# One matmul per key block for the exponents of two heads: mask, key part and running maximum in one operand, split on ScalarE and GpSimd and laid out through DRAM, with new orders on the engines

## The chip, the cores and the metric

The kernel runs on one core of one Trainium2 chip. The metric is the device time of one execution in microseconds. The kernel before takes 1728.18 us, the median of 3 runs (1726.94 to 1734.21).

## What is computed

Input x is (128, 256, 512) and a context of the same shape: 128 batches of 256 positions and 512 features, 8 heads of 64. A layer norm of x gives the queries; keys and values are the context itself. The first layer is a gated linear attention:

```python
ig, fg = gi @ igate_w.T + igate_b, gi @ fgate_w.T + fgate_b   # gi = [q, k, v]
cs = cumsum(log_sigmoid(fg))
log_D = where(tril, cs[:, None] - cs[None, :], -inf) + ig[None, :]
D = exp(log_D - max(log_D, -1))
C = (q @ k.T / 8) * D
h = (C / (max(|sum C|, exp(-max)) + 1e-6)) @ v
x = x + layernorm_per_head(h) * out_w
x = x + fp8_gemm(layernorm(x)) + bias
```

With a = ig - cs per key and a running maximum mx of a per query, the exponent of D for a key and a later query is a(key) - mx(query), and it is masked where the key comes after the query. These exponents, for each head, are what the change makes in another way.

## The kernel before, in words

The batches go through a software pipeline. Every engine has a function slot(m), called for m from FIRST to B + LAST, which issues one piece of each stage for batches m - 4 to m + 10; the engines don't share a clock, they are tied by semaphores only, and each works its slot's list in the order in which it is written. One period is the time in which every engine does the work of one batch.

What one batch needs, with the lines of the profile:

- SP issues all DMAs (the context c_sb and its halves c_first, the keys kT, x twice: for the norm, x_sb, and for the residual, into o_sb; store writes o_sb out, L336). load_own (L304) loads x into the buffer that the output leaves from, so it waits until the store of two batches earlier has landed, and all of SP's queue behind it waits with it.
- ScalarE normalises x; TensorE turns it (turn, L391), ScalarE keeps it as qT; gates (L402) gives the gate sums.
- Once per group of four batches the scans run, on 32 rows (4 batches x 8 heads) of 256 columns: scan_rows on TensorE (L416), abs, exp, log, relu on ScalarE, three scans and a few sums on VectorE. am holds a in columns 0 to 255 and mx in 256 to 511. scan_rest (L1048, VectorE, twice per group) takes from am its upper 16 bits and then again, so that rows 0 to 31, 32 to 63 and 64 to 95 hold three pieces of which each fits in bf16: a sum of three bf16 operands gives the fp32 value.
- arg(b, q), on TensorE, four times per batch, makes the exponents of two heads in one PSUM bank: 14 bf16 matmuls (L445 to L457) in three kinds. am is the stationary operand and the head's selector hsel the moving one for a; hsel_neg is stationary and am moving for -mx; ident_bf and the table later add -1e30 where the key comes after the query. Operands of 64 columns come in pairs (low and high half of the output partitions) that run side by side.
- ScalarE takes the exponential (decay, L613), VectorE multiplies it with the scores (matrix, L909, from scores, L476), TensorE multiplies that with the values (within, L508), adds what comes across the two halves (across, L520; states, L488), VectorE adds and normalises per head (L916 to L955), GpSimd scales and adds the residual (head_norm L1143, scale_heads L1156, residual L1161; weigh_keys L1134 weights the keys for states).
- The second norm (L963 to L980), its bf16 turn (L531), the quantisation to fp8 on ScalarE (quantise, L746, once per batch), the feed-forward product in the one PSUM bank y (ffn, L545 and L547, twice per batch) and finish (L1003, VectorE, after each of the two).

At the start SP loads the first four batches and the weights; VectorE then rounds the feed-forward weights (L847 to L867) between its first slots and waits for w_out before it.

The few lines that carry the stages:

```python
mm(low[:, :, 0:2, :], tops[:, 0:Q], two, start=True, stop=False)            # arg, L445, a of the lower keys
mm(low[:, h, 0:2, :], neg, tops[:, S:S + 2 * Q], start=False, stop=False)   # L451, -mx
mm(low[:, :, 0::2, :], ident_bf[:, 0:Q], later..., start=False, stop=True)  # L455, the mask
tt(am[(n + 1) * R:(n + 2) * R, g, :], rows, top, ALU.subtract)              # scan_rest, L1048
```

## Time and profile before

| | |
|---|---|
| median of 3 runs | 1728.18 us (1726.94 to 1734.21) |
| the profiled execution | 1743.25 us |
| its span | 1741.5 us |
| TensorE busy | 1598.6 us, 92% |
| VectorE busy | 1548.9 us, 89% |
| ScalarE busy | 1282.7 us, 74% |
| GpSimd busy | 1104.4 us, 63% |
| moved by DMA | 377.66 MB, mean 217 GB/s |

The span is the time from the first to the last instruction of one execution; the profiled execution's own time is 1.75 us more. Busy counts a moment once, also when two instructions of an engine overlap in it. Shares are over the whole span, fill and drain included, so that windows of the steady middle tell more. A row of the trace gives the start and the duration of an instruction; TensorE's matmuls are pipelined, and the distance from start to start is what one costs. PE is TensorE, PEld its weight load, DVE VectorE, ACT ScalarE, POOL GpSimd, SPq SP's queue of DMA issues.

### The profile page before, as it was taken

Reading aid. Unit: us, or ns where it says so; the run is one execution under the profiler, and the core shown is the slowest. Engines: PE = TensorE matmul, PEld = TensorE weight load, DVE = VectorE, ACT = ScalarE, POOL = GpSimd, SP = SyncE. Lnnn points to the kernel's source line nnn. Section 1 sums busy time; section 2 is a strip of 40 time slices with the busy share of each in tenths; the row PEclk is TensorE's granted clock in tenths of the full one; section 3 lists DMA queues with packets and bytes.
Section 4 is the critical chain, followed back from the end, with each engine's and each line's share of the span. In section 5 each row is a group of like instructions: output and inputs, shape, how many; then the busy total and the mean of one; then the engine's idle time right before and its main releaser. Section 6 shows DMA issues by size and latency. Waiting matters only on the chain.

```text
span 1741.5 us, 88634 instructions
## 1 busy us (share of the span) xinstructions
PE 1598.6 (92%) x36224; PEld 1191.2 (68%) x36224; DVE 1548.9 (89%) x4157; ACT 1282.7 (74%) x3137; POOL 1104.4 (63%) x1036
## 2 busy tenths in 40 slices
PE   2779999999999999999999999999999999999985
PEld 1567777776777776777776767777777777777662
DVE  6679999999998999999999999999999899998884
ACT  3667877777787777777877778777777787777652
POOL 0056766666666666666666667766666666666774
PEclk9899999999999999999999999999999999999996
DMA  5557778777777677677776777778778777776542
GB/s 164 198 168 220 249 222 237 222 230 231 224 237 233 218 234 226 214 240 221 238 235 216 227 233 227 244 217 246 218 225 240 216 223 241 230 232 195 179 130 73
DMA packets 164022, 377.66 MB, mean 217 GB/s; under 512 B 15008, under 2 KB 16032, under 8 KB 163616
## 3 DMA queue, kind: packets, MB, share of 16 engines
q1 hardware_dynamic: 163616, 371.96, 69.2%
q8 instruction: 290, 4.75, 1.1%
q14 instruction: 116, 0.95, 0.2%
HBM read 304.79 MB, written 67.11 MB: 214 GB/s over the span
## 4 chain that ended last, share of the span: by engine, by line
PE 58%; DVE 21%; issue 9%; DMA 9%; ACT 2%; POOL 1%; DVEq 0%; SPq 0%; POOLq 0%; ACTq 0%
PE work L508 9%; PE y L547 9%; PE qk L476 8%; PE turn L391 6%; PE turn L402 5%; DMA o_sb<-in_x 5%; DVE dec L909 4%; DMA out<-o_sb 3%; DVE bn L963 3%; DVE o_sb L1003 3%; PE arg L445 3%; PE work L488 3%; PE y L531 2%; PE y L545 2%; DVE am L1048 2%
## 5 line engine op out<-in xcount | busy, mean ns | idle before, releaser
L1143 POOL TENSOR_TENSOR x<-x,h_r 128x512 f32<-128x512 f32 x256 | 269.3, 1052 | 261.4 <-DVE x L955 146.0
L1156 POOL TENSOR_TENSOR x<-x,w_out 128x512 f32<-128x512 f32 x256 | 360.2, 1407 | 20.1
L1161 POOL TENSOR_TENSOR x<-x,o_sb 128x512 f32<-128x512 f32 x256 | 321.2, 1276 | 38.5 <-DMA o_sb<-in_x 38.2
L508 PEld LDWEIGHTS work<-c_first,dec 128*64 128x64 f32 x4096 | 264.7, 138 | 69.2 <-issue 69.0
L508 PE MATMUL work<-c_first,dec 128*64 128x65 f32 x4096 | 290.9, 224 | 12.2 <-issue 4.8
L508 PE MATMUL work<-c_sb,dec 128*64 128x65 f32 x4096 | 292.3, 224 | 2.4 <-issue 2.3
L508 PEld LDWEIGHTS work<-c_sb,dec 128*64 128x64 f32 x4096 | 264.7, 138 | 5.3 <-issue 5.3
L476 PE MATMUL qk<-qT,kT 64*64 64x128 f32 (+1 forms) x8192 | 236.0, 250 | 34.6 <-DVE dec L909 28.6
L547 PE MATMUL y<-w_ffn,zq 128*128 128x512 bf16 x1024 | 267.2, 384 | 0.0
L1003 DVE SCALAR_TENSOR_TENSOR o_sb<-y,s_out,x 128x512 f32<-128x512 f32 x256 | 190.4, 744 | 78.1 <-PE y L547 77.2
L613 ACT ACTIVATE dec<-arg 128x384 f32<-128x384 f32 x512 | 243.2, 475 | 19.4 <-PE arg L457 18.7
L909 DVE TENSOR_TENSOR dec<-qk,dec 128x768 f32<-128x768 f32 x256 | 242.8, 948 | 8.0 <-PE qk L476 8.0
L476 PEld LDWEIGHTS qk<-qT,kT 64*64 64x64 f32 x8192 | 198.9, 133 | 69.0 <-issue 41.3
L946 DVE BATCH_NORM_STATS2 bn_h<-g_sb 128x6 f32<-128x128 f32 x1024 | 224.0, 280 | 0.0
L649 ACT ACTIVATE q_nat<-x_sb,nb,r 128x512 f32<-128x512 f32 x256 | 205.5, 806 | 0.0
L738 ACT ACTIVATE z_bf<-x,nb,r 128x512 bf16<-128x512 f32 x256 | 194.5, 807 | 14.2 <-DVE nb L980 11.3
L391 PE MATMUL turn<-ident,q_nat 128*128 128x128 f32 x1024 | 173.5, 293 | 28.9 <-ACT q_nat L649 19.3
L963 DVE BATCH_NORM_STATS2 bn<-x 128x6 f32<-128x512 f32 x256 | 174.5, 681 | 18.4 <-POOL x L1161 18.0
L746 ACT ACTIVATE zq<-y,s_inv 128x1024 fp8e4<-128x1024 bf16 x128 | 142.5, 1113 | 59.9 <-PE y L531 59.9
L885 DVE BATCH_NORM_STATS2 bn<-x_sb 128x6 f32<-128x512 f32 x256 | 174.6, 683 | 13.5 <-DMA x_sb<-in_x 6.7
L955 DVE TENSOR_TENSOR x<-g_sb,bn_h 128x512 f32<-128x512 f32 x256 | 183.1, 715 | 1.0
L601 ACT ACTIVATE qT<-turn 128x512 f32<-128x512 f32 x256 | 151.5, 592 | 36.9 <-PE turn L391 31.7
(120 smaller groups left out, 4547.8 us busy)
## 6 DMA issues: line engine op xcount, KB each, us to landing
c_sb<-in_ctx SPq DMA_DIRECT2D x128, 520.0 KB, 6.2
x_sb<-in_x SPq DMA_DIRECT2D x128, 512.0 KB, 5.1
kT<-in_keys SPq DMA_DIRECT2D x128, 512.0 KB, 6.6
o_sb<-in_x SPq DMA_DIRECT2D x128, 512.0 KB, 4.6
out<-o_sb SPq DMA_DIRECT2D x128, 512.0 KB, 3.1
c_first<-in_ctx SPq DMA_DIRECT2D x256, 130.0 KB, 5.3
w_ffn<-in_L_ffn_kernel SPq DMA_DIRECT2D x1, 512.0 KB, 10.1
w_out<-in_L_xattn_out_w SPq DMA_DIRECT2D x1, 256.0 KB, 11.7
```

What stands on the lines that cost most here:

```text
L391: last = turn(turn_ps[:, (T * c + t) * P:(T * c + t + 1) * P], q_nat[:, t, chunk * P:(chunk + 1) * P], ident[:, :])
L476: last = mm(out[0:Q, u, to, :] if lower else out[Q:P, u, to, :], kT[half, r, c, key * Q:(key + 1) * Q], qT[half, r, c, query * Q:(query + ...
L508: last = mm(work_ps[rows, u, c * W:(c + 1) * W], heads_dec[:, slot * Q:(slot + 1) * Q], src, start=True, stop=True)
L547: last = mm(y_ps, (zq_wide if wide_z else zq)[:, c, t * P:(t + 1) * P], w_ffn[:, c, :], start=False, stop=c == C - 1)
L613: af(dec[:, b.k % 2, q, :], arg_ps[:, 0:U * HEAD], ACT.Exp).then_inc(decays[q].sem, 1)
L909: tt(mine, qk_ps[:, :, 0:U * HEAD], mine, ALU.mult).then_inc(weighted[p].sem, 1)
L946: done = ve.bn_stats(bn_h[:, first:first + U, :].rearrange("p u k -> p (u k)"), g_sb[:, b.k % 2, t, c, 1:1 + U * DH].rearrange("p (u d) -> ...
L963: done = ve.bn_stats(bn2[:, t, :], x1[:, b.k % 2, t, :])
L1003: stt(o_sb[:, b.k % 2, t, :], y_ps, s_out[:, :], x1[:, b.k % 2, t, :], ALU.mult, ALU.add).then_inc(out_set[t].sem, 1)
L1143: pl.tensor_tensor(h, h, h_r[:, t * NH:(t + 1) * NH].unsqueeze(2).broadcast_to([P, NH, DH]), ALU.mult).then_inc(h_normed[t].sem, 1)
L1156: pl.tensor_tensor(h, h, w_out[:, :], ALU.mult).then_inc(h_scaled[t].sem, 1)
L1161: pl.tensor_tensor(x1[:, b.k % 2, t, :], x1[:, b.k % 2, t, :], o_sb[:, b.k % 2, t, :], ALU.add).then_inc(x1_set[t].sem, 1)
```

## The change

1. Three pieces of a and mx are now made once per group by ScalarE and GpSimd: parts_high (ScalarE copies am to bf16), scan_rest (GpSimd subtracts), parts_middle (ScalarE copies), parts_low (GpSimd subtracts). VectorE's scan_rest is gone, am has 32 rows.
2. SP stores the pieces to DRAM, once per group with four DMAs (store_parts): the keys' as they are, the queries' into an image in which a head's piece stands only in its own columns, and other heads' columns stay zero. Per batch it loads both back (load_parts): 24 rows of 256 (arg_keys) and 24 rows of 3072 (arg_queries), two buffers of each.
3. The operands for arg have 112 rows: 64 with the identity against the mask, 24 with a's pieces against ones in the head's own columns, 24 with -1 against mx's pieces. One matmul of a key block does what three kinds did, so arg is 4 matmuls instead of 14.
4. At the start SP loads the constant rows of both buffers, and the images in DRAM are filled from the same table; SP waits for these six DMAs before it issues the feed-forward weights.
5. The orders of all five slots are new, and FIRST and LAST are one further out on either side.

```diff
-FIRST, LAST = -10, 4
+FIRST, LAST = -11, 5
...
-        am = sb("am", [P, 2, 2 * S])
+        am = sb("am", [R, 2, 2 * S])
+        rest = sb("rest", [R, 2 * S])
+        parts = sb("parts", [R, 3, 2 * S], bf16)
+        arg_keys = sb("arg_keys", [ROWS, PART_RING, S], bf16)
+        arg_queries = sb("arg_queries", [ROWS, PART_RING, NH, SPAN], bf16)
+        key_parts = nc.dram_tensor("key_parts", (2, GROUP, NH, 3, S), bf16).ap()
+        query_parts = nc.dram_tensor("query_parts", (2, GROUP, IMAGE), bf16).ap()
...
+            def store_parts(b):
+                g = b.k // GROUP % 2
+                sp.wait_ge(*parts_set.of(b))
+                if b.follows(2 * GROUP):
+                    for last in range(1, PART_RING + 1):
+                        before = b - (GROUP + last)
+                        sp.wait_ge(parts_in[before.k % PART_RING], before.count(32, 32, PART_RING))
+                sp.dma_start(key_parts[g, :, :, :, :].rearrange("j h n s -> (j h) n s"), parts[:, :, 0:S]).then_inc(parts_stored, 16)
+                for to, at, n in ((0, 0, S), (S, Q, Q), (S + Q, 3 * Q, Q)):
+                    sp.dma_start(own_columns(g, to, n), parts[:, :, S + at:S + at + n]).then_inc(parts_stored, 16)
+
+            def load_parts(b):
+                r, g, j = b.k % PART_RING, b.k // GROUP % 2, b.k % GROUP
+                sp.wait_ge(parts_stored, b.count(N_PARTS, N_PARTS, GROUP))
+                if b.follows(PART_RING):
+                    sp.wait_ge(*args[3].of(b - PART_RING))
+                sp.dma_start(arg_keys[KEY_ROWS, r, :], key_parts[g, j, :, :, :].rearrange("h n s -> (h n) s")).then_inc(parts_in[r], 16)
+                sp.dma_start(arg_queries[QUERY_ROWS, r, :, :].rearrange("p h s -> p (h s)"),
+                             image(g, j)).then_inc(parts_in[r], 16)
 
...
+            for r in range(PART_RING):
+                sp.dma_start(arg_keys[:, r, :], c_keys).then_inc(blank_in, 16)
+                sp.dma_start(arg_queries[:, r, :, :].rearrange("p h s -> p (h s)"), c_queries).then_inc(blank_in, 16)
+            for g in range(2):
+                sp.dma_start(query_parts[g, :, 0:PARTS * NH * SPAN],
+                             c_queries[QUERY_ROWS, :].rearrange("p n -> (p n)").unsqueeze(0).broadcast_to([GROUP, PARTS * NH * SPAN])).then_inc(blank_in, 16)
+            sp.wait_ge(blank_in, N_BLANK)
...
             def slot(m):
+                if live(m - 5):
+                    store(m - 5)
+                if live(m + 6):
+                    load_keys(m + 6)
+                if scans(m):
+                    store_parts(m)
+                if live(m - 1):
+                    load_first(m - 1)
+                if live(m - 3):
+                    load_own(m - 3)
+                if live(m):
+                    load_parts(m)
+                if live(m + 2):
+                    load_c(m + 2)
                 if live(m + 10):
                     load_x(m + 10)
-                if live(m - 2):
-                    load_own(m - 2)
-                if live(m + 7):
-                    load_keys(m + 7)
-                if live(m + 1):
-                    load_first(m + 1)
-                if live(m + 3):
-                    load_c(m + 3)
-                if live(m - 3):
-                    store(m - 3)
 
...
             def arg(b, q):
-
-                j, g = b.k % GROUP, b.k // GROUP % 2
-                row = j * NH + 2 * U * (q // U) + q % U
-                tops = am[:, g, :].bitcast(bf16).rearrange("p (s two) -> p s two", two=2)[:, :, 1]
-                mine = hsel[:, row:row + U + 1:U]
+                r = b.k % PART_RING
+                first = 2 * U * (q // U) + q % U
+                mine = slice(first, first + U + 1, U)
                 out = arg_ps[:, 0:U * HEAD].rearrange("p (h s n) -> p h s n", h=2, s=3)
                 low, high = out[0:Q], out[Q:P]
                 if q == 0:
-                    pe.wait_ge(*rest_set[1].of(b))
-                    if not b.follows(1):
-                        pe.wait_ge(dve_set, N_SCAN_SET)
+                    pe.wait_ge(parts_in[r], b.count(32, 32, PART_RING))
                     if b.follows(1):
                         pe.wait_ge(*decays[3].of(b - 1))
                 else:
                     pe.wait_ge(*decays[q - 1].of(b))
-                two = mine.unsqueeze(2).unsqueeze(3).broadcast_to([P, 2, 2, Q])
-                one = mine.unsqueeze(2).broadcast_to([P, 2, Q])
-                mm(low[:, :, 0:2, :], tops[:, 0:Q], two, start=True, stop=False)
-                mm(high[:, :, 0::2, :], tops[:, 2 * Q:3 * Q], two, start=True, stop=False)
-                mm(low[:, :, 2, :], tops[:, 3 * Q:4 * Q], one, start=False, stop=False)
-                mm(high[:, :, 1, :], tops[:, Q:2 * Q], one, start=False, stop=False)
-                for h in range(2):
-                    neg = hsel_neg[:, row + U * h:row + U * h + 1].broadcast_to([P, Q])
-                    mm(low[:, h, 0:2, :], neg, tops[:, S:S + 2 * Q], start=False, stop=False)
-                    mm(high[:, h, 0::2, :], neg, tops[:, S + 2 * Q:S + 4 * Q], start=False, stop=False)
-                    mm(low[:, h, 2, :], neg, tops[:, S + 3 * Q:S + 4 * Q], start=False, stop=False)
-                    mm(high[:, h, 1, :], neg, tops[:, S + Q:S + 2 * Q], start=False, stop=False)
-                mm(low[:, :, 0::2, :], ident_bf[:, 0:Q], later[:, 0:Q].unsqueeze(1).unsqueeze(2).broadcast_to([P, 2, 2, Q]),
-                   start=False, stop=True)
-                mm(high[:, :, 0:2, :], ident_bf[:, Q:P], later[:, Q:P].unsqueeze(1).unsqueeze(2).broadcast_to([P, 2, 2, Q]),
-                   start=False, stop=True).then_inc(args[q].sem, 1)
+                tops = arg_queries[:, r, mine, :].rearrange("p h (s n) -> p h s n", n=Q)
+                mm(low[:, :, 0:2, :], arg_keys[:, r, 0:Q], tops[:, :, 0:2, :], start=True, stop=True)
+                mm(high[:, :, 0::2, :], arg_keys[:, r, 2 * Q:3 * Q], tops[:, :, 2:4, :], start=True, stop=True)
+                mm(low[:, :, 2, :], arg_keys[:, r, 3 * Q:4 * Q], tops[:, :, 5, :], start=True, stop=True)
+                mm(high[:, :, 1, :], arg_keys[:, r, Q:2 * Q], tops[:, :, 4, :], start=True, stop=True).then_inc(args[q].sem, 1)
 
...
             def slot(m, wide_z):
+                if live(m + 2):
+                    arg(m + 2, 3)
+                if live(m - 1):
+                    ffn(m - 1, 0, wide_z)
+                if live(m + 9):
+                    turn_round(m + 9, 0)
+                if live(m + 2):
+                    states(m + 2)
+                if live(m - 1):
+                    ffn(m - 1, 1, wide_z)
+                if live(m + 9):
+                    turn_round(m + 9, 1)
                 if live(m + 3):
                     arg(m + 3, 0)
-                if scans(m + 3):
-                    scan_turn(m + 3)
-                if live(m + 9):
-                    turn_round(m + 9, 1)
-                if live(m - 1):
-                    ffn(m - 1, 1, wide_z)
                 if live(m + 2):
...
+            def parts_high(b):
+                act.wait_ge(*max_set.of(b))
+                if b.follows(GROUP):
+                    act.wait_ge(parts_stored, b.count(N_PARTS, 0, GROUP))
+                af(parts[:, 0, :], am[:, b.k // GROUP % 2, :], ACT.Copy).then_inc(high_set.sem, 1)
+
+            def parts_middle(b):
+                act.wait_ge(*rest_set.of(b))
+                af(parts[:, 1, :], rest[:, :], ACT.Copy).then_inc(middle_set.sem, 1)
...
-            def scan_rest(b, n):
-
-                g = b.k // GROUP % 2
-                dve.wait_ge(*(rest_set[0] if n else max_set).of(b))
-                if b.follows(2 * GROUP):
-                    dve.wait_ge(*args[3].of(b - (GROUP + 1)))
-                rows = am[n * R:(n + 1) * R, g, :]
-                top = rows.bitcast(bf16).rearrange("p (s two) -> p s two", two=2)[:, :, 1]
-                tt(am[(n + 1) * R:(n + 2) * R, g, :], rows, top, ALU.subtract).then_inc(rest_set[n].sem, 1)
...
+            def scan_rest(b):
+                pool.wait_ge(*high_set.of(b))
+                if b.follows(GROUP):
+                    pool.wait_ge(*parts_set.of(b - GROUP))
+                pl.tensor_tensor(rest[:, :], am[:, b.k // GROUP % 2, :], parts[:, 0, :], ALU.subtract).then_inc(rest_set.sem, 1)
+
+            def parts_low(b):
+                pool.wait_ge(*middle_set.of(b))
+                pl.tensor_tensor(parts[:, 2, :], rest[:, :], parts[:, 1, :], ALU.subtract).then_inc(parts_set.sem, 1)
...
             def slot(m):
                 if live(m + 7):
+                    scale_heads(m + 7, 0)
+                    scale_heads(m + 7, 1)
+                if scans(m + 11):
+                    scan_rest(m + 11)
+                if live(m + 8):
+                    head_var(m + 8)
+                if live(m + 7):
+                    residual(m + 7, 0)
                     residual(m + 7, 1)
+                if scans(m + 11):
+                    parts_low(m + 11)
                 if live(m + 10):
                     weigh_keys(m + 10)
                 if live(m + 8):
                     head_norm(m + 8, 0)
-                    scale_heads(m + 8, 0)
                     head_norm(m + 8, 1)
-                    scale_heads(m + 8, 1)
-                if live(m + 9):
-                    head_var(m + 9)
-                if live(m + 8):
-                    residual(m + 8, 0)
 
...
+    block, parts = P // 2, 3 * n_heads
+    own = np.repeat(np.eye(n_heads, dtype=np.float32), 3, axis=0)
+    earlier = np.where(np.arange(block)[:, None] > np.arange(block)[None, :], np.float32(-1e30), np.float32(0))
+    keys = np.zeros((block + 2 * parts, 4, block), np.float32)
+    keys[:block] = np.eye(block, dtype=np.float32)[:, None, :]
+    keys[block + parts:] = -1
+    queries = np.zeros((block + 2 * parts, n_heads, 6, block), np.float32)
+    for masked in (0, 2, 4, 5):
+        queries[:block, :, masked, :] = earlier[:, None, :]
+    queries[block:block + parts] = own[:, :, None, None]
```

TensorE, in the steady run, from the second transpose of a batch over the first feed-forward half to arg. Before (the names: turn is the transposes' and gates' bank, y the feed-forward's, work the states'):

```order
L391 MATMUL turn<-ident,q_nat 128x128 x4
L545 MATMUL y<-b_parts,b_rows 128x512
L547 MATMUL y<-w_ffn,zq 128x512 x4
L488 MATMUL work<-c_sb,k_w 64x65 x8
L445 MATMUL arg<-hsel,am 64x2x128
L446 MATMUL arg<-hsel,am 64x2x2x64
L447 MATMUL arg<-hsel,am 64x2x64
L448 MATMUL arg<-hsel,am 64x2x64
L451 MATMUL arg<-am,hsel_neg 64x128
L452 MATMUL arg<-am,hsel_neg 64x2x64
L453 MATMUL arg<-am,hsel_neg 64x64
L454 MATMUL arg<-am,hsel_neg 64x64
```

Six more rows of arg follow there. Now:

```order
L581 MATMUL y<-b_parts,b_rows 128x512
L583 MATMUL y<-w_ffn,zq 128x512 x4
L442 MATMUL turn<-ident,q_nat 128x128 x4
L524 MATMUL work<-c_sb,k_w 64x65 x8
L581 MATMUL y<-b_parts,b_rows 128x512
L583 MATMUL y<-w_ffn,zq 128x512 x4
L442 MATMUL turn<-ident,q_nat 128x128 x4
L491 MATMUL arg<-arg_queries,arg_keys 64x2x128
L492 MATMUL arg<-arg_queries,arg_keys 64x2x2x64
L493 MATMUL arg<-arg_queries,arg_keys 64x2x64
L494 MATMUL arg<-arg_queries,arg_keys 64x2x64
```

arg is whole in these four rows. The first call of a batch now comes after both feed-forward halves, and between the two halves stand a transpose and the states.

SP, the slot in which a group's pieces are stored. Before, a slot was:

```order
L336 DMA out_0<-o_sb 128x2x512
L295 DMA x_sb<-in_x 128x2x512
L304 DMA o_sb<-in_x 128x2x512
L320 DMA kT<-in_keys 128x1024
L332 DMA c_first<-in_ctx 64x520 x2
L314 DMA c_sb<-in_ctx 128x1040
```

Now, once per group (in the other three slots L362 and L364 are missing):

```order
L377 DMA out_0<-o_sb 128x2x512
L341 DMA kT<-in_keys 128x1024
L362 DMA key_parts<-parts 96x1x256
L364 DMA query_parts<-parts 32x3x256
L364 DMA query_parts<-parts 32x3x64 x2
L353 DMA c_first<-in_ctx 64x520 x2
L325 DMA o_sb<-in_x 128x2x512
L371 DMA arg_keys<-key_parts 24x256
L372 DMA arg_queries<-query_parts 24x3072
L335 DMA c_sb<-in_ctx 128x1040
L316 DMA x_sb<-in_x 128x2x512
```

The loads of the pieces come behind the residual's load, and so behind the landing of the store at the top.

GpSimd, the same group's slot, now (h_r, w_out and o_sb name head_norm, scale_heads and residual):

```order
L1197 TENSOR_TENSOR x1<-x1,w_out 128x512 x2
L1174 TENSOR_TENSOR rest<-am,parts 32x512
L1192 TENSOR_TENSOR h_v<-h_n2,bn_h 128x16
L1202 TENSOR_TENSOR x1<-x1,o_sb 128x512 x2
L1178 TENSOR_TENSOR parts<-rest,parts 32x512
L1165 TENSOR_TENSOR k_w<-c_sb,facs 128x512
```

The two subtractions (L1174, L1178) stand ahead of the keys' weighting and around the residual; the rest of the slot is as long as it was.

## Rows read from the trace of the kernel before

**Rows 1.** Page: the span; busy us of each engine (share of the span) xinstructions.

```profile
span 1741.5 us, 88634 instructions
...
PE 1598.6 (92%) x36224; PEld 1191.2 (68%) x36224; DVE 1548.9 (89%) x4157; ACT 1282.7 (74%) x3137; POOL 1104.4 (63%) x1036
```

**Rows 2.** Windows, 400 to 1472 us: busy us per engine, granted clock, DMA share.

```profile
core 0: us, PE busy (x) PEld busy (x) DVE busy (x) ACT busy (x) POOL busy (x), PEclk, DMA share, GB/s
400.00:1472.00 1072.00, 1023.57 (x23634) 769.62 (x23629) 991.29 (x2672) 831.75 (x2043) 717.03 (x668) 1.00 0.75 229
```

**Rows 3.** Line L746 between 600 and 1100 us: count, duration, first and last start.

```profile
L746 ACT ACTIVATE zq<-y,s_inv x39: 1113/1113/1115, 599.5 to 1088.4; 128x1024 fp8e4<-128x1024 bf16 x39
```

**Rows 4.** Waits, 400 to 1472 us: us in total, times, longest.

```profile
PE qk L476 <- DVE dec L909: 18.9, 18, 1.1
...
DVE o_sb L1003 <- PE y L547: 39.4, 46, 2.2
```

**Rows 5.** Timeline of TensorE: start us, duration us, what; one call of arg.

```profile
814.35 0.27 PE L445 MATMUL arg<-hsel,am 128*64 128x256 bf16 x1
...
814.46 0.22 PE L447 MATMUL arg<-hsel,am 128*64 128x128 bf16 x1
...
814.52 0.22 PE L451 MATMUL arg<-am,hsel_neg 128*64 128x128 bf16 x1
...
814.70 0.27 PE L455 MATMUL arg<-later,ident_bf 128*64 128x256 bf16 x1
...
814.90 0.90 PE L476 MATMUL qk<-qT,kT 64*64 64x128 f32 x32
```

**Rows 6.** VectorE's subtractions: group (busy, mean ns), then least, median, greatest ns.

```profile
L1048 DVE TENSOR_TENSOR am<-am 32x512 f32<-32x512 f32 x64 | 75.2, 1175 | 2.0
...
L1048 DVE TENSOR_TENSOR am<-am x64: 680/702/1799, 60.5 to 1652.2; 32x512 f32<-32x512 f32 x64
```

**Rows 7.** Timelines of VectorE and of GpSimd at 829 us.

```profile
829.52 1.79 DVE L1048 TENSOR_TENSOR am<-am 32x512 f32<-32x512 f32 x1
...
829.49 1.28 POOL L1156 TENSOR_TENSOR x<-x,w_out 128x512 f32<-128x512 f32 x1
```

**Rows 8.** Groups: finish on VectorE, and those nearest to the added operations; busy, mean ns.

```profile
L1003 DVE SCALAR_TENSOR_TENSOR o_sb<-y,s_out,x 128x512 f32<-128x512 f32 x256 | 190.4, 744 | 78.1 <-PE y L547 77.2
...
L601 ACT ACTIVATE qT<-turn 128x512 f32<-128x512 f32 x256 | 151.5, 592 | 36.9 <-PE turn L391 31.7
...
L1134 POOL TENSOR_TENSOR k_w<-c_sb,facs 128x512 f32<-128x512 f32 x128 | 133.7, 1044 | 70.3 <-ACT facs L697 62.4 <-PE work L488 7.9
...
L1161 POOL TENSOR_TENSOR x<-x,o_sb 128x512 f32<-128x512 f32 x256 | 321.2, 1276 | 38.5 <-DMA o_sb<-in_x 38.2
```

**Rows 9.** Timeline of SP's queue: start us, time to issue, what.

```profile
814.26 0.40 SPq L336 DMA_DIRECT2D out<-o_sb  x1
...
817.30 0.37 SPq L304 DMA_DIRECT2D o_sb<-in_x  x1
```

**Rows 10.** Waits of SP, 400 to 1472 us.

```profile
SPq L304 <- DMA out<-o_sb: 203.1, 84, 4.5
```

**Rows 11.** Page, DMA issues: KB each, median us from issue to landing.

```profile
kT<-in_keys SPq DMA_DIRECT2D x128, 512.0 KB, 6.6
...
out<-o_sb SPq DMA_DIRECT2D x128, 512.0 KB, 3.1
c_first<-in_ctx SPq DMA_DIRECT2D x256, 130.0 KB, 5.3
```

**Rows 12.** The fill: a window, VectorE's wait and first maximum, ScalarE's first exponential.

```profile
12.00:22.00 10.00, 2.05 (x8) 1.43 (x8) 6.50 (x22) 3.30 (x8) 0.00 (x0) 1.00 0.90 320
...
21.59 0.41 DVE L847 MEMSET b_rows<- 1x128 bf16 x2 [1.23 <-DMA w_out<-in_L_xattn_out_w]
...
59.16 0.66 DVE L1028 TENSOR_TENSOR_SCAN am<-am 32x256 f32<-32x256 f32 x1
...
66.36 0.49 ACT L613 ACTIVATE dec<-arg 128x384 f32<-128x384 f32 x1 [0.22 <-PE arg L457]
```

174 lines of the change are left out of this document (86 added, 88 removed).

## The prediction, before the change was run

> **What bounds the kernel now.** I read the page first: on the whole span TensorE is busy 92% and VectorE 89% [rows 1]. An average over fill, steady run and drain does not say which of the two sets the pace, so the next view was a window over the steady middle: 1072 us in which TensorE ran at its full granted clock (1.00 of 2.4 GHz) and the DMA engines were busy 0.75 of the time [rows 2]. One ScalarE operation happens once per batch (the quantisation); 39 of them start between 599.5 and 1088.4 us, so a batch takes 488.9 / 38 = 12.87 us [rows 3] and the window holds 1072 / 12.87 = 83.3 batches. Per batch the engines are then busy: TensorE 1023.57 / 83.3 = 12.29 us, VectorE 991.29 / 83.3 = 11.90, ScalarE 9.98, GpSimd 8.61 [rows 2]. So TensorE is the limit with 0.58 us of idle time a batch, and VectorE stands only 0.39 us behind it. The waits agree: VectorE's largest wait in that window is for TensorE's feed-forward product, 39.4 us or 0.47 a batch, while TensorE's largest, for VectorE, is 18.9 us [rows 4]. 128 batches at 12.87 are 1647 us; the other 94 us of the span are fill and drain.
>
> **TensorE: the exponents.** Today each of the four calls of arg per batch is 14 matmuls. In the timeline the call starts at 814.35, its third matmul (after the first pair of 256 columns) at 814.46, the last pair at 814.70, and the next operation starts at 814.90: 0.55 us [rows 5]. The change keeps the first pair (0.11 us) and one pair of 128 columns, after which the scores follow. That last pair costs at least the 0.06 us of a pair of 128 columns between its neighbours, and at most the 0.20 us that the last pair of 256 now takes before the scores; I take 0.14. The call then takes 0.25, and saves 0.30 us; four of them save **1.2 us a batch**, bounds 0.24 x 4 = 0.96 and 0.38 x 4 = 1.5. TensorE's need falls from 12.29 to about 11.1 us. It is no longer the limit, so this is not the gain.
>
> **VectorE: the splits go away.** scan_rest was two subtractions per group of four batches, 64 in all, 75.2 us, mean 1175 ns [rows 6]. Over 128 batches that is **0.59 us a batch**. VectorE's need falls from 11.90 to 11.3 us, and it becomes the limit. Nothing else on it is removed; the other moves only reorder. That the mean is 1175 and the shortest 680 ns [rows 6] is worth a look: one of 1.79 us started 0.03 us after a GpSimd multiplication that ran 1.28 us [rows 7]. The subtraction sat waiting for GpSimd. The Trainium skill (SBUF — State Buffer, Who interferes with whom) says that VectorE's second port pair is shared with GpSimd as an exclusive lock, taken for a whole instruction, also against VectorE operations with two SBUF inputs. The trace agrees.
>
> **ScalarE and GpSimd take the splits over.** Two copies of 32x512 per group on ScalarE: a Copy of 128x512 takes 592 ns, so 2 x 0.6 / 4 = 0.3 us a batch, to 10.3. Two subtractions on GpSimd, between the 1044 and the 1276 ns of its 512-element operations [rows 8]: 0.52 to 0.64, taken as 0.58, to 9.2 us. Both stay more than 1 us below VectorE, and I cost them at nothing; if they hit VectorE through the port of rows 7, that is a rival below.
>
> **DMA and SP's queue.** Each batch adds loads of 24x512 bytes and 24x6144 bytes, 160 KB, and each group four stores, about 123 KB: 0.19 MB on top of 2.9 MB. DMA busy time of 0.75 x 12.87 = 9.6 us [rows 2, 3] becomes about 10.2; at a 12 us batch that is 0.85 of the time. No limit, but the landings will hardly be shorter, and the piece of 147 KB sits on 24 partitions only, with its share of the engines unknown: evenly spread it adds 0.34 us to each, if a third of the engines carry it 1 us to those. The serial path counts more. On SP, the part loads of batch b stand behind: the store of b-5 (0.40 us), the residual load, which waits until that store has landed (3.1), its issue (0.37), and two issues of their own (0.4 each) [rows 9, 11]. SP already waits so: 203.1 us in the window for the store's landing [rows 10]. With VectorE's 0.74 us to finish b-5 [rows 8], and a landing L of the parts, arg(b, 0), about one period later on TensorE, asks for a period of at least 0.74 + 0.40 + 3.1 + 0.37 + 0.8 + L = 5.4 + L. The nearest row for L is the load of c_first, 130 KB, 5.3 us [rows 11]: 10.7 us, hidden. For the first batch of a group four stores (1.6 us to issue) and the wait for their landing come in between: 12.3 us, just late, and more if GpSimd's last piece comes late itself. For this and for landings above 5.3 us I charge **0.2 us a batch**, between 0 (all hidden) and what rival D gives.
>
> **The period.** No engine runs without waits here: today the limiting one idles 0.58 us per batch. I give VectorE the same: 11.3 + 0.58 + 0.2 = **12.1 us**. From below 11.3 bounds it; from above nothing here does, and the rivals say what would push it up. 128 x (12.87 - 12.1) = **-99 us**.
>
> **The fill gets longer.** SP now issues six loads of constants, the masked blanks, and waits for all of them before the feed-forward weights. They are 2 x (57 + 688) KB into SBUF and 2 x 590 KB within DRAM, 2.7 MB; the DMA engines moved 320 GB/s at 12 to 22 us, at 0.90 busy [rows 12]. So 8.4 us, plus a landing and the weights' own way after it, about 3: **+11 us**. Today VectorE's next step in the fill waits for w_out until 21.59 us [rows 12], so the delay counts in full. Less than 5 is excluded by the bytes; if the copies within DRAM go at half that rate, it is 15. The first group's splits then go ScalarE, GpSimd, ScalarE, GpSimd (0.6 + 1.05 + 0.6 + 1.05), DRAM stores (1.6 to issue, 3.1 to land) and loads (0.8 + 3 to 5): 12 to 14 us after the first running maximum at 59.16 + 0.66, so about 73 us. The first exponential starts now at 66.36 [rows 12]: **+7 us**. Together +18, bounds +8 and +30.
>
> **Sum**: -99 + 18 = -81 us. Against the profiled execution, 1743.25 us (span 1741.5 and 1.75 around it), that is 1662; the profiled run stands 15 us above the median of 1728.18, so for the median **1647 us**.
>
> **Rivals.**
> (A) VectorE hardly waits: TensorE, with 1.8 us more than it needs, always has its product ready. For it: 0.47 of today's 0.97 us of VectorE idle is waiting for that product [rows 4]. Against it: y is one bank, so finish and product still alternate. Period 11.5, fill +12: 1728 - 175 + 12 = 1565 us.
> (B) GpSimd gives it back. Its 0.58 us a batch of new subtractions each hold up a VectorE operation as in rows 7; at worst in full. Period 11.3 + 0.58 + 0.58 = 12.5: 1728 - 47 + 18 = 1699 us. For it: rows 7. Against it: the old subtraction, which suffered from the same, is gone. The rule of the Trainium skill named above asks for this case if its lock meets two-input operations each time.
> (C) The gain is swallowed whole: the once-a-group work of TensorE, ScalarE and VectorE now lies in different slots, and if each of them waits for the other's, their times add rather than overlap. 11.3 with 1.45 us of idle is 12.75: 1728 - 15 + 18 = 1731 us. Nothing in today's trace shows so much idle time.
> (D) **Slower**: the parts come late for every batch. This is SP's path with L as the one unknown: it decides against today's kernel from L = 12.87 - 5.4 = 7.5 us on. For it: the keys' load, 512 KB, has a median of 6.6 us [rows 11], the DMA engines become busier, and only 24 partitions hold the whole piece. At L = 8.3 the period is 13.7: 1728 + 106 + 18 = 1852 us. Against it: 130 KB took 5.3, and what stands in the queue ahead has mostly landed during SP's wait. The Trainium skill (SBUF — State Buffer, Door 1: the DMA port swizzle) states a rule that speaks for D: a transfer reaches only the ports that its partitions belong to, and by its table partitions 88 to 111 are six of sixteen. An estimate by that page: 147 KB / 6 = 24.6 KB for each of six engines, on top of some 180, so these would be busy 11 us or more of each batch, and the queues in front of them long. No run here shows the spread yet; the one load of 64 partitions, c_first, takes 5.3 us for a quarter of the bytes that the keys' takes 6.6 for.
>
> **Chances.** The forecast (1605 to 1690) 0.50; A 0.10; B 0.22; C 0.06; D 0.12. A measurement of this kernel tells about 0.5%, 8.6 us, from no change. Faster by more: 0.82; within it: C, 0.06; slower: D, 0.12. The range leaves out D and the lower half of A (periods under 11.6): 1575 to 1732 us.
>
> **What would show it.** Right: quantisations 12.1 us apart in the steady middle (11.8 to 12.4); arg at about 0.25 us from its start to the next operation; TensorE busy near 11.1 and VectorE near 11.3 us a batch, VectorE now the busier one; landing of the query parts under 6 us, and nearly no TensorE wait for them but one in four; VectorE's wait in the fill until about 33 us. Wrong: TensorE waits with the DMA of the parts as the releaser in every batch (D); GpSimd's or VectorE's two-input operations with means well above today's (B); VectorE idle above 1 us a batch with waits spread over slots (C); a period still near 12.9 with TensorE busy 12.3, which would mean that the small matmuls were not what took the time.

## The result, and the profile after

The changed kernel takes 1738.84 us (median of 20 runs), the kernel before 1733.32 in the same session: ratio **1.0037, 95% interval 1.0020 to 1.0055**. By the ratio that is 6.4 us slower (5.5 by the medians), less than the 0.5% that was called no change. The prediction was 1647 us and faster. All comparisons below are ratios to the kernel before on the same chip, since its median moved between 1727 and 1738 us from chip to chip; differences in us are differences of these ratios, and 1% is 17.3 us. Between runs on different chips the plain medians can give another size; where that matters, both are given.

The profiled execution took 1734.2 us (span 1732.4), 5 us under its own median, while the profiled one of before stood above its median; so this pair of profiles shows 9 us of gain where the medians show a loss of 6. Against [rows 1], the page:

```profile
span 1732.4 us, 79000 instructions
...
PE 1491.7 (86%) x31104; PEld 1073.4 (62%) x31104; DVE 1509.6 (87%) x4091; ACT 1311.8 (76%) x3201; POOL 1139.2 (66%) x1097
```

The window over the steady middle, against [rows 2], and the quantisations, against [rows 3]:

```profile
400.00:1472.00 1072.00, 973.61 (x20684) 707.64 (x20683) 980.23 (x2678) 867.81 (x2129) 754.84 (x723) 1.00 0.81 248
```

```profile
L793 ACT ACTIVATE zq<-y,s_inv x40: 1114/1115/1116, 607.1 to 1096.3; 128x1024 fp8e4<-128x1024 bf16 x40
```

In this stretch a batch takes 489.2 / 39 = 12.54 us. The 85 quantisations of the whole window (406.3 to 1465.8 us) are 12.61 us apart, so the window holds 85.0 batches: TensorE 11.46 us, VectorE 11.53, ScalarE 10.21, GpSimd 8.88. TensorE's busy time fell by 0.8 us (12.29 before; 1.2 forecast), VectorE's by 0.4 (11.90 before; 0.6 forecast), and VectorE now idles 1.08 us a batch.

A window is not the run, though. Over all 128 quantisations (groups of the two lines; before, then now) the distance is 12.73 us before and 12.51 now, 0.22 less, where the stretches of [rows 3] gave 0.33: 127 times 0.22 is 27 us, and the fill takes 18 of them back, which is the 9 us of this pair.

```profile
L746 ACT ACTIVATE zq<-y,s_inv x128: 1113/1113/1115, 114.7 to 1730.9; 128x1024 fp8e4<-128x1024 bf16 x128
```

```profile
L793 ACT ACTIVATE zq<-y,s_inv x128: 1114/1115/1117, 133.0 to 1721.8; 128x1024 fp8e4<-128x1024 bf16 x128
```

The call of arg shrank as forecast. What a call costs depends on what follows it. Where the scores follow, as in [rows 5], 0.55 us became 0.29 (825.39 to 825.68). Where the product with the values follows, it is now 0.19 us (824.26 to 824.45); before, such calls took 0.48:

```profile
824.26 0.30 PE L491 MATMUL arg<-arg_queries,arg_keys 112*64 112x256 bf16 x1
...
824.39 0.22 PE L494 MATMUL arg<-arg_queries,arg_keys 112*64 112x128 bf16 x1
824.45 0.22 PE L544 MATMUL work<-c_first,dec 128*64 128x65 f32 x1
...
825.39 0.30 PE L491 MATMUL arg<-arg_queries,arg_keys 112*64 112x256 bf16 x1
...
825.68 0.90 PE L512 MATMUL qk<-qT,kT 64*64 64x128 f32 x32
```

Three things in the trace stand out against the kernel before; what each is worth, the experiments have to say. First, VectorE's subtraction for the exponentials of the scans, 403 ns in the kernel before, now runs beside GpSimd's (timelines of VectorE and of GpSimd; group of the line: busy, mean ns):

```profile
825.47 1.49 DVE L1087 TENSOR_TENSOR ex<-ncs,am 32x256 f32<-32x256 f32 x1
```

```profile
825.53 1.15 POOL L1178 TENSOR_TENSOR parts<-rest,parts 32x512 bf16<-32x512 f32 x1
```

```profile
L1087 DVE TENSOR_TENSOR ex<-ncs,am 32x256 f32<-32x256 f32 x32 | 46.7, 1460 | 0.0
```

Second, DMAs land late. Of the waits in the window, these name a load (us in total, times, longest):

```profile
POOL x L1202 <- DMA o_sb<-in_x: 31.6, 31, 2.9
...
PEld arg L491 <- DMA arg_queries<-query_parts: 10.5, 14, 2.3
...
PE arg L491 <- DMA arg_queries<-query_parts: 7.4, 8, 2.0
```

The last two rows are the same moments twice, once for the weight load and once for the matmul behind it: 14 of the window's 85 first calls waited for the query parts, 10.5 us in all. The residual's x was waited for before too (22.1 us, 21 times).

Third, the fill. VectorE's wait for w_out, which ended at 21.59 us before [rows 12], ends at 41.75, behind the blanks (timeline of VectorE, and the chain that ended last):

```profile
41.75 0.66 DVE L895 MEMSET b_rows<- 1x128 bf16 x3 [21.71 <-DMA w_out<-in_L_xattn_out_w]
```

```profile
10.88 24.72 DMA query_parts<-in_c_queries
36.61 5.07 DMA w_out<-in_L_xattn_out_w
```

The first of the 128 quantisations starts at 132.99 us, 18.3 later than before (114.69). From the last one to the end it is 10.6 us in both.

### The profile page after: what moved, and what is told of

Same layout as the page of the kernel before. It is cut to its first block, busy times and chain, and to the rows that moved or that the text cites. A ratio compares the mean times of both kernels' runs of the same rounds, so it can differ in the third digit from the quotient of the medians.

```text
span 1732.4 us, 79000 instructions
## 1 busy us (share of the span) xinstructions
PE 1491.7 (86%) x31104; PEld 1073.4 (62%) x31104; DVE 1509.6 (87%) x4091; ACT 1311.8 (76%) x3201; POOL 1139.2 (66%) x1097
## 4 chain that ended last, share of the span: by engine, by line
PE 36%; DVE 24%; issue 15%; DMA 10%; ACT 8%; POOL 3%; SPq 3%; DVEq 0%; ACTq 0%; POOLq 0%
PE y L583 7%; PE work L544 6%; DMA o_sb<-in_x 4%; DVE dec L957 4%; DVE bn L1011 3%; PE qk L512 3%; PE turn L453 3%; PE y L567 3%; ACT zq L793 3%; PE y L581 3%; DVE o_sb L1051 3%; PE turn L442 2%; DVE bn_h L994 2%; DMA arg_queries<-query_parts 2%; POOL x L1202 2%
## 5 line engine op out<-in xcount | busy, mean ns | idle before, releaser
L544 PE MATMUL work<-c_first,dec 128*64 128x65 f32 x4096 | 286.4, 223 | 44.0 <-DVE carry L964 40.2
L1197 POOL TENSOR_TENSOR x<-x,w_out 128x512 f32<-128x512 f32 x256 | 321.3, 1277 | 0.0
L544 PEld LDWEIGHTS work<-c_first,dec 128*64 128x64 f32 x4096 | 260.5, 138 | 64.2 <-issue 62.5
L650 ACT ACTIVATE dec<-arg 128x384 f32<-128x384 f32 x512 | 247.4, 483 | 23.6 <-PE arg L494 22.8
L544 PEld LDWEIGHTS work<-c_sb,dec 128*64 128x64 f32 x4096 | 260.6, 138 | 1.2 <-issue 1.1
L512 PE MATMUL qk<-qT,kT 64*64 64x64 f32 (+1 forms) x8192 | 239.9, 251 | 17.6 <-issue 16.7
L638 ACT ACTIVATE qT<-turn 128x512 f32<-128x512 f32 x256 | 152.0, 594 | 124.5 <-PE turn L442 123.4
L442 PE MATMUL turn<-ident,q_nat 128*128 128x128 f32 x1024 | 162.5, 283 | 59.6 <-ACT q_nat L686 53.5
L442 PEld LDWEIGHTS turn<-ident,q_nat 128*128 128x128 f32 x1024 | 131.9, 146 | 113.2 <-ACT q_nat L686 57.2
L1011 DVE BATCH_NORM_STATS2 bn<-x 128x6 f32<-128x512 f32 x256 | 169.8, 682 | 23.9 <-POOL x L1202 23.5
L1003 DVE TENSOR_TENSOR x<-g_sb,bn_h 128x512 f32<-128x512 f32 x256 | 182.1, 711 | 0.5 <-issue 0.5
```

What stands on the lines that cost most here:

```text
L442: last = turn(turn_ps[:, (T * c + t) * P:(T * c + t + 1) * P], q_nat[:, t, chunk * P:(chunk + 1) * P], ident[:, :])
L512: last = mm(out[0:Q, u, to, :] if lower else out[Q:P, u, to, :], kT[half, r, c, key * Q:(key + 1) * Q], qT[half, r, c, query * Q:(query + ...
L544: last = mm(work_ps[rows, u, c * W:(c + 1) * W], heads_dec[:, slot * Q:(slot + 1) * Q], src, start=True, stop=True)
L650: af(dec[:, b.k % 2, q, :], arg_ps[:, 0:U * HEAD], ACT.Exp).then_inc(decays[q].sem, 1)
L1011: done = ve.bn_stats(bn2[:, t, :], x1[:, b.k % 2, t, :])
L1197: pl.tensor_tensor(h, h, w_out[:, :], ALU.mult).then_inc(h_scaled[t].sem, 1)
```

## The experiments

**What is the removed work worth?** Three versions of the kernel before.

b_four, the calls of arg:
```diff
-                mm(low[:, :, 0:2, :], tops[:, 0:Q], two, start=True, stop=False)
...
+                mm(low[:, :, 0:2, :], ident_bf[:, 0:Q], two, start=True, stop=True)
+                mm(high[:, :, 0::2, :], ident_bf[:, Q:P], two, start=True, stop=True)
+                mm(low[:, :, 2, :], ident_bf[:, 0:Q], one, start=True, stop=True)
+                mm(high[:, :, 1, :], ident_bf[:, Q:P], one, start=True, stop=True).then_inc(args[q].sem, 1)
```


> The kernel before with TensorE's relief alone: each exponent call issues four matmuls with the changed kernel's column counts (the identity as weights, so that the running maximum and the mask are left out of the exponents) in place of fourteen; VectorE, GpSimd, the DMAs and all orders stay. Theory TensorE (the matmuls' length sets the period together with VectorE, as the prediction's sum has it): 1.2 us a batch less on TensorE, but VectorE's 11.90 stays, so the period goes from 12.87 to some 12.5 and the run falls by about 50 us (40 to 60). Theory VectorE (TensorE had slack, its waits only move): less than 20 us.

b_norest, VectorE's slots (and arg waits for max_set):
```diff
-                if scans(m + 1):
-                    scan_rest(m + 1, 0)
...
-                    scan_rest(m + 1, 1)
```


> The kernel before with VectorE's relief alone: the two subtractions scan_rest of each group are left out (the exponents lack their middle and low pieces), nothing replaces them. Theory TensorE: TensorE's 12.29 stays, so the run falls by at most 20 us. Theory VectorE: 0.59 us a batch of VectorE's path goes, 128 times: the run falls by 40 to 75 us.

b_both, both edits:

> Both reliefs in the kernel before, with no GpSimd work, no DMA and no new order beside them (exponents without pieces, running maximum and mask). It is what the change removes, without what it adds. The prediction's steady term (12.87 to 12.1) says about 100 us less. If the removed work was worth less than that, the prediction's sum failed in what it took away; if it is 100 us or more, it failed in what the change adds.

Measured: b_four 1705.27 us, ratio 0.9805 (0.9776 to 0.9835), -34 us; b_norest 1712.52, 0.9842 (0.9813 to 0.9871), -27 us; b_both 1643.92, **0.9456 (0.9424 to 0.9487), -94 us**. The two together are worth 33 us more than their sum: with one engine relieved the other holds the period. Each alone is below what the theory of its own engine gave it (40 to 60, 40 to 75), and above the other theory. The window of b_both, and its wait for the residual's x:

```profile
400.00:1472.00 1072.00, 1007.07 (x21320) 716.30 (x21316) 981.66 (x2761) 871.74 (x2148) 763.43 (x702) 0.99 0.77 240
```

```profile
POOL x L1147 <- DMA o_sb<-in_x: 51.2, 34, 3.3
```

Its 88 quantisations in the window (399.6 to 1463.9 us) are 12.23 us apart, which gives VectorE 11.20 us a batch and 1.03 idle. The chain that ended last points to where much of that idle time comes from: in this window 14.8% of it is the load of the residual's x and 8.4% the store that this load waits for, against 3.2% and nothing listed in the kernel before; VectorE's own wait for the residual rose from 7.7 to 31.6 us. Of the 94 us about 7 are fill (first quantisation 108.0 against 114.7). So the change removes nearly what the prediction's steady term needed, and **all of it is given back by what the change adds and moves: 101 us** from b_both (0.9456) to the changed kernel (1.0037).

**Is TensorE's saving still used?** a_thrice issues the four matmuls three times:

> The changed kernel with each exponent call's four matmuls issued three times over into the same place (same result): TensorE gets back 0.5 us a call, 2 us a batch, 256 us in all. If TensorE is still what the batches wait for, the run grows by more than 150 us; if VectorE sets the period now and TensorE has its 1.15 us a batch of slack, by the 0.85 us a batch that goes beyond the slack, some 110 us or less. This tells how much of TensorE's saving the changed kernel still uses.

Measured: 1781.05, ratio 1.0237 (1.0209 to 1.0266), 35 us above the changed kernel. The expectation took 0.5 us more a call; the trace has 0.33 (a call before the product with the values takes 0.52 us in place of 0.19), so some 170 us of matmuls came in, and TensorE's busy time rose from 11.46 to 12.42 us a batch. Only 35 us show, 9 of them in the fill (first quantisation 142.2). So TensorE's matmuls do not set the period of the changed kernel. What is left is the busiest engine, VectorE, with its waits; a_exp and a_expool below take work from it.

**What does the change give back?** First the fill, a_wfirst:
```diff
+            sp.dma_start(w_ffn[:, :, :], ffn_w.rearrange("(c p) f -> p c f", p=P)).then_inc(weights_in, 16)
...
             for r in range(PART_RING):
                 sp.dma_start(arg_keys[:, r, :], c_keys).then_inc(blank_in, 16)
...
-            sp.wait_ge(blank_in, N_BLANK)
-            sp.dma_start(w_ffn[:, :, :], ffn_w.rearrange("(c p) f -> p c f", p=P)).then_inc(weights_in, 16)
```
SP waits for the blanks only ahead of the first store of parts.

> The changed kernel with the feed-forward weights, their bias and the output weights issued ahead of the DRAM images' blanks; SP waits for the blanks only ahead of the first store of parts. Theory fill (VectorE's 21.7 us wait for w_out until 41.75 is the fill's limit): w_out lands as before, near 30 us, and the run falls by 11 to 18 us. Rival (the first group's round trip through DRAM, arg at 94.0, sets the start whatever lands earlier): under 5 us.

Then the loads of the parts, a_noparts:
```diff
-                sp.wait_ge(parts_stored, b.count(N_PARTS, N_PARTS, GROUP))
                 if b.follows(PART_RING):
-                    sp.wait_ge(*args[3].of(b - PART_RING))
+                    return
+                sp.wait_ge(parts_stored, b.count(N_PARTS, N_PARTS, GROUP))
```
store_parts no longer waits for earlier loads, and arg waits only for the first two.

> The changed kernel without the loads of the key and query parts after the first two batches (all exponents are then made of the parts of those two): 252 of its DMAs gone, the stores into the DRAM image stay. Theory DMA (the parts' traffic and their lateness, with the residual's load that comes late by them, give back the gain): the waits for own_in and for the parts go, and the run falls by 40 to 80 us. Rival (the two-input clash of GpSimd and VectorE and the once-a-group work do it): under 15 us.

a_exp, VectorE's slots:
```diff
-                if scans(m + 1):
-                    scan_exponents(m + 1)
...
                 if scans(m + 2):
                     scan_max(m + 2)
+                    scan_exponents(m + 2)
```


> The changed kernel with VectorE's scan_exponents right behind scan_max, one batch earlier, where GpSimd makes no subtraction. If the clash of the two engines is what stretches its subtraction from 403 to 1460 ns, the mean of the line returns to about 400 to 600 ns, worth 1.0 us a group and up to 32 us in all if VectorE sets the period; by the theory that DMAs set it, under 8 us.

a_nosplit, GpSimd's slots:
```diff
-                if scans(m + 11):
-                    scan_rest(m + 11)
...
-                    parts_low(m + 11)
```
ScalarE's parts_middle copies am in place of rest.


> The changed kernel without GpSimd's two subtractions a group (the middle piece is a copy of the high one and the low one stays zero); ScalarE's copies, the stores, the loads and the orders stay. Theory port (GpSimd's 74 us of subtractions hold up VectorE's two-input operations and GpSimd's own chain to the residual): the run falls by 25 to 60 us. Theory DMA: under 15 us.

Measured: a_wfirst 0.9998 (0.9975 to 1.0021), 7 us under the changed kernel, with intervals that just touch, so between the two theories; in the trace the fill is 12 us shorter (first quantisation 121.08). a_noparts 0.9876 (0.9853 to 0.9899), 28 us under it, also between the theories; a_exp 1.0054 (1.0027 to 1.0081), no gain; a_nosplit 0.9994 (0.9968 to 1.0019), 7 us under it, with intervals that all but touch. The loads are the largest of these items, though below the 40 to 80 of theory DMA. The port theory falls in size: without any of GpSimd's subtractions only 7 us come back. This is no full test of it, since VectorE's L1087 still takes 1049 ns on average in a_nosplit, now beside the weighting of the keys (started at 632.96 us, for 1.17, while that ran from 632.80 for 1.04). And a_exp shows why moving the clash does not help. Its two groups (busy, mean ns):

```profile
L1003 DVE TENSOR_TENSOR x<-g_sb,bn_h 128x512 f32<-128x512 f32 x256 | 206.0, 805 | 0.5 <-issue 0.5
L1087 DVE TENSOR_TENSOR ex<-ncs,am 32x256 f32<-32x256 f32 x32 | 12.9, 402 | 0.0
```

scan_exponents is back at 402 ns, 34 us less of VectorE's time, and the centring of the heads, L1003, took 24 us more (711 ns before the move). Of the 169 in the window 20 took over 1 us, about one a group, and 19 of these started while GpSimd's weighting of the keys (L1164 there) ran.

The same subtraction handed to GpSimd, a_expool:
```diff
+                pl.tensor_tensor(ex[:, 0:S], ncs[:, :], am[0:R, b.k // GROUP % 2, S:2 * S], ALU.subtract).then_inc(exponents.sem, 1)
```
VectorE's own is gone from scan_exponents.

> The changed kernel with the subtraction of scan_exponents made by GpSimd, behind weigh_keys, where GpSimd waits 0.84 us for VectorE; the negated maximum stays on VectorE under a semaphore of its own. VectorE loses 1.46 us a group. Theory VectorE (its clashes set the undisturbed group of 48.1 us): the run falls by 30 to 45 us. Rival (as with scan_exponents moved one batch earlier: another two-input operation of VectorE takes the clash, or the chain waits elsewhere): within 10 us of the changed kernel.

Measured: 1743.45, 1.0053 (1.0023 to 1.0084). The rival held: VectorE's busy time in the window fell to 954.5 us, and the time went into its waits. So VectorE's busy time alone does not set the period either.

**The new orders without the additions**, a_bare (GpSimd's, ScalarE's and SP's added steps deleted from their slots, arg waits for max_set and for the blanks):

> The changed kernel with its new orders and its four matmuls a call, but without all that the change adds: no copies of pieces on ScalarE, no subtractions on GpSimd, no stores or loads of parts (the exponents are then the mask alone); the blanks stay, ahead of the weights. Beside the kernel before without fourteen-matmul calls and without scan_rest (1644 us) it differs by the orders and the fill alone. Theory additions (splits and parts cost what the gain is missing): about 1655 to 1665, the 12 us of the later weights above it. Rival (the new orders themselves are worse, by VectorE's scan_exponents that stays near 1050 ns and by its place): 1680 to 1700.

Measured: 1692.86, 0.9739 (0.9705 to 0.9773). Closer to the rival: 51 us of the 101 are there with no part split, stored or loaded. Two follow-ups took it apart, a_bare_w with the weights first (the diff of a_wfirst) and a_bare_l with the blanks issued six slots later as well:

> The changed kernel's orders and matmuls without its additions, as before (1693 us), with the feed-forward weights issued ahead of the blanks. If the late weights are the fill's cost, it falls by 12 to 20 us, to about 1677, and what stays above 1644 (the old orders with the same work) is the new orders' own cost of some 30 us. If it stays at 1685 or more, the fill's length has another cause in the orders.

```diff
             def slot(m):
+                if m.k == -5:
+                    for r in range(PART_RING):
+                        sp.dma_start(arg_keys[:, r, :], c_keys).then_inc(blank_in, 16)
```


> The changed kernel's orders and matmuls without its additions and with the weights first (1666 us, 0.966 of before), now with the blanks issued six slots later, behind the loads of x for the first batches. In the trace with the blanks only behind the weights, a load of x lands 20.8 us late, at 40.7 us. Theory blanks (their 2.7 MB hold up every load of the start, not the weights alone): the run falls by 8 to 14 us, and what is left above the old orders with the same work (0.946) is under 1%. Theory orders (the start is longer because of the new slots): under 3 us.

Measured: a_bare_w 0.9657 (0.9618 to 0.9697), 14 us under a_bare; a_bare_l 0.9632 (0.9596 to 0.9668), 4 us less again, within the intervals. The chain of a_bare_w in the fill shows what was left after the first edit, a load of x that VectorE waits for until 40.70 us. In a_bare_l SP issues that load at 20.05 us, and VectorE starts on it at 32.65 without a wait; the next one, issued at 33.55, takes 8.4 us. The first quantisations stand at 131.99 (a_bare), 121.04 and 114.76 us:

```profile
19.87 20.81 DMA x_sb<-in_x
```

The later blanks are visible in the trace (6 us) and not clear of the noise in the time: neither the 8 to 14 us of theory blanks nor a refutation. From b_both (0.9456) to a_bare_l it is still 1.8%, 30 us, where theory blanks left under 1%. The two do nearly the same work in two orders (a_bare_l also loads the blanks, and its arg reads the 112-row operands): 7 us of it are fill (first quantisation of b_both: 108.0).

**Bytes or latency of the query parts?** a_pairs:
```diff
-                sp.dma_start(arg_queries[QUERY_ROWS, r, :, :].rearrange("p h s -> p (h s)"),
-                             image(g, j)).then_inc(parts_in[r], 16)
+                for i in range(NH // 2):
+                    first = QUERY_ROWS.start + 6 * i
+                    sp.dma_start(arg_queries[first:first + 6, r, 2 * i:2 * i + 2, :].rearrange("p h s -> p (h s)"),
+                                 image(g, j)[6 * i:6 * i + 6, 2 * i * SPAN:(2 * i + 2) * SPAN]).then_inc(parts_in[r], 16)
```


> The changed kernel with the query parts of a batch loaded by four DMAs of six rows and two heads' columns each, in place of one of 24 rows and all eight heads' columns (the rest of the rows stays zero from the blanks): a quarter of its 147 KB, three more DMAs a batch. Theory bytes (leaving both loads out was worth 28 us through the DMA engines' share): the run falls by 12 to 25 us. Theory count (what costs is each DMA's issue and latency in SP's queue): no gain, or slower by up to 20 us.

a_double:
```diff
+                sp.dma_start(again[Q + PARTS * (1 - r):Q + PARTS * (2 - r), :], image(g, j)).then_inc(parts_in[r], 16)
```


> The changed kernel with each batch's query parts (147 KB) loaded a second time, into a tile that nothing reads, on the semaphore that the exponents wait for. Theory bytes (a quarter of these bytes gave 34 us back): their worth is about 45 us for all of them, so the run grows by 35 to 60 us. Theory width (what the wide load cost was its own latency ahead of the exponents, not its share of the DMA engines): under 15 us more.

a_eights, as a_pairs but eight loads `arg_queries[first:first + 3, r, h, :]`:

> The changed kernel with the query parts in eight loads of three rows and one head's columns (768 B a row, 18 KB in all) in place of one load; four loads of 37 KB gave 1705 us. Theory bytes: 18 KB less than four loads are worth 5 us at most, the count costs nothing while SP has 12 us a batch: 1698 to 1708. Theory count: four more DMAs a batch on SP's queue cost more than that: 1710 or more.

Measured: **a_pairs 1704.74, 0.9820 (0.9792 to 0.9848), 38 us under the changed kernel**; a_double 1.0411 (1.0372 to 1.0451), 65 us above it; a_eights 0.9920 (0.9886 to 0.9953), 17 us worse than four loads. So the wide load costs what its width costs, and eight small ones cost more than four (by the plain medians, on two chips, 7 us and not 17). Why is open: SP waits for ScalarE ahead of the load of x only 11.7 us in the window of a_eights, against 80.7 in a_pairs and 124.5 in the changed kernel, but for the landing of the store 101.2 us against 59.8 in a_pairs, and in all it still waits a third of the time, so its queue is not full.

a_pairs and a_double lie beyond the ranges of theory bytes (12 to 25, 35 to 60), on the side of a greater effect. And narrowing the load gave 10 us more than leaving out both loads did in a_noparts (5 by the plain medians; the batches of their traces are 12.32 us apart in both). So the narrow loads cost nothing that can be told from noise, and what the loads cost is the wide one's width, 28 to 38 us. What the wide load holds up is read in the waits. Of a_pairs:

```profile
POOL x L1204 <- DMA o_sb<-in_x: 14.4, 21, 2.0
...
PEld arg L493 <- DMA arg_queries<-query_parts: 0.3, 1, 0.3
```

and of a_double:

```profile
POOL x L1204 <- DMA o_sb<-in_x: 48.3, 39, 3.3
PEld arg L493 <- DMA again<-query_parts: 48.1, 42, 3.5
...
PE arg L493 <- DMA again<-query_parts: 38.6, 31, 3.3
```

31.6 us of waiting for the residual's x become 14.4 and 48.3, and TensorE's 14 waits for the parts (10.5 us) become one (0.3) and 42 (48.1 us; as above, the rows of PE are the same moments again). On the chain that ended last the residual's load is 4.7% of this window in the changed kernel and not among the lines listed for a_pairs. That is how these runs differ; it does not show that each us of such waiting costs a us, since b_both, the fastest of all, waited 51.2 us for the residual's x. The windows of a_pairs and of a_double give the DMA share:

```profile
400.00:1472.00 1072.00, 987.26 (x21072) 719.17 (x21070) 995.89 (x2729) 881.15 (x2169) 768.19 (x737) 1.00 0.78 243
```

```profile
400.00:1472.00 1072.00, 946.70 (x19911) 686.95 (x19909) 941.34 (x2576) 835.32 (x2042) 728.21 (x695) 0.99 0.85 251
```

**Do the gains add up?** They join the single edits from above: a_all (a_pairs, a_wfirst, a_expool), a_pw (a_pairs, a_wfirst) and a_pwl (a_pw with the blanks six slots later):

> The changed kernel with three edits: feed-forward weights issued ahead of the blanks, query parts in four small loads, scan_exponents' subtraction on GpSimd. By the sum of the theories (fill 7 to 12, bytes 12 to 25, VectorE 30 to 45) some 1665 to 1690 us, below both kernels; by the rivals 1725 to 1745.

> The changed kernel with two edits, query parts in four small loads and the feed-forward weights issued ahead of the blanks; scan_exponents as in the change. If the two gains (34 us, 8 to 12 us) add up: 1690 to 1698, the fastest correct version. If the weights' place is worth nothing once the loads are small: 1702 to 1708.

> The fastest correct version so far (query parts in four small loads, weights ahead of the blanks, 0.977 of before) with the blanks issued six slots later as well. Theory blanks: 8 to 14 us less, about 0.970 of before; theory orders: under 3 us less; if the first group's parts now wait for the blanks, slower.

Measured: a_all 1706.52, 0.9829 (0.9797 to 0.9861), in neither of its ranges; a_pw 1685.93, 0.9767 (0.9734 to 0.9800), 9 us under a_pairs, so two gains add up; a_pwl 1686.50, **0.9712 (0.9680 to 0.9744)**. That a_all is 11 us above a_pw can only lie in its third edit, the subtraction on GpSimd, or in the two chips. a_pw and a_pwl do the change's whole work and beat both kernels, by 2.3% and 2.9%. Whether a_pwl beats a_pw the intervals, which overlap at their ends, leave nearly open.

## Why the prediction was wrong

The account of the 101 us, in ratios: new orders 1.8% (b_both to a_bare_l, 30 us); blanks ahead of the weights and of the first loads 1.1% (to a_bare, 18 us); splits, stores and narrow loads 0.8% (a_bare to a_pairs, 14 us); the width of the query load 2.2% (38 us). Against the forecast of -81 us the result, +6, is 87 us off. Three steps of the prediction account for it, to rounding: the relief came out 33 us smaller (-127 to -94), the new orders cost 30 us where nothing was charged, and splits and parts cost 52 us where 26 were charged.

- **TensorE and VectorE's relief: mechanism right, size too large.** Without the 0.2 us charge the steady term was 12.87 to 11.88 us, -127 us; b_both, which is just that, gave -94, and some 7 of these are fill. The step that failed is "I give VectorE the same" 0.58 us of idle. That was TensorE's idle; VectorE's own was 0.97 before and is 1.03 in b_both (its busy time, 11.20, is near the forecast 11.3). What the sum left out is SP's older path: the faster batches wait for the store's landing and the residual's load, together 23% of b_both's chain. That this path is what keeps VectorE's idle time at 1.03 is read from the chain and the waits, and no run tests it. The call of arg was costed right: 0.29 us before the scores against 0.25 forecast, and 0.27 to 0.29 us saved a call against 0.30. TensorE's busy time fell less than the calls did, 0.8 us against 1.1; that difference stays open.
- **"The other moves only reorder": wrong, 30 us costed at nothing.** That they cost is shown by b_both against a_bare_l, nearly the same work in two orders. Where is only partly seen: 7 us in the fill, and scan_exponents, 403 ns on average in b_both and 860 in a_bare_l, 15 us of VectorE's time, though a_exp and a_expool show that taking such time away need not shorten the run. VectorE's waits moved rather than shrank: for the residual from 31.6 to 1.1 us in the window, but for TensorE's feed-forward product from 34.3 to 57.8, and for ScalarE in the second norm from 6.1 to 20.8. Which of the moves does it stays open.
- **DMA and SP's queue: the term that was mis-sized.** I charged 0.2 us a batch, 26 us, and nothing for the splits. Splits, stores and loads together cost 52: the wide load 28 to 38 of them, the subtractions on GpSimd about 7. The DMA busy time was forecast right (10.2 us a batch; 0.81 x 12.61 = 10.2 measured), and so was that TensorE waits for the parts in less than one batch of four (14 of 85). What I left out is that this load makes the others late: with it, against the four small ones, GpSimd's waits for the residual's x are 31 against 21 (31.6 us against 14.4), and c_sb's median landing is 5.8 us against 4.5 (6.2 in the kernel before). How these add up to 38 us is not shown.
- **Rival D** named the right place with too high a price. In the steady part the load's landings on the chain are 4.3 to 6.7 us, under the 7.5 at which D begins. Of the rule in the Trainium skill (SBUF — State Buffer, Door 1: the DMA port swizzle) the runs show this much: the second copy in a_double raised the DMA busy time from 10.2 to 0.85 x 13.07 = 11.1 us a batch, 0.9 for 147 KB, where all 3.13 MB took 10.2. By engine time these bytes were 1.9 times as dear as the mean (1.6 to 2.1 by the rounding of the shares alone), and the 0.34 us that the prediction gave for an even spread was too low even for mean bytes, which come to 0.48. That agrees with a load that few ports share, but no view shows the engines one by one, so the cause of the factor is open.
- **Rival B** was seen and small. VectorE's L1087 went from 403 to 1460 ns, with the exclusive lock of the Trainium skill (SBUF — State Buffer, Who interferes with whom), which the prediction had named, as the likely reason. The new orders alone, with no subtraction on GpSimd at all, took it to 860 and 915 ns (a_bare_l, a_bare). Removing the subtractions gave 7 us, and moving the clash none.
- **The fill: the size right by luck, the reason half wrong.** +18 forecast, +18.3 measured at the first quantisation. But the 7 us for the splits' round trip through DRAM are 1 us (132.99 with it, 131.99 in a_bare without). The blanks cost 17 (131.99 to 114.76), not 11: w_out came 20 us later (41.75 against 21.59), since the last copy within DRAM alone takes 24.72 us of the chain, where 8.4 was worked out for all six; and the blanks held up the loads of x too. And the relief and the new orders, which the forecast of the fill left out, gave 7 us (114.7 to 108.0) and took 7 (to 114.8). At the first exponential, the point that the forecast itself used, the delay is 28 us (66.4 to 94.6).

## What to carry over

Before counting on a relief, make the kernel that has the relief alone: b_both would have said 94 us, and set the budget for everything that is added. Here a matmul operand that is mostly zeros was cheap on TensorE (0.19 us a call) and dear to load (28 to 38 us): keep the zeros resident and load only the blocks that change, and not in more pieces than that needs (four did better than eight). Loads of constants belong behind whatever the fill waits for.
